# Cross attention's 154 keys in parts of 128 and 26 instead of 77 and 77

## The reference

```
qh = (x @ wq.T + bq).reshape(Bx, N, H, d).transpose(0, 2, 1, 3)
kh = (memory @ wk.T + bk).reshape(Bx, -1, H, d).transpose(0, 2, 1, 3)
vh = (memory @ wv.T + bv).reshape(Bx, -1, H, d).transpose(0, 2, 1, 3)
a = jax.nn.softmax(jnp.einsum('bhnd,bhmd->bhnm', qh, kh) / jnp.sqrt(jnp.float32(d)), axis=-1)
ca = jnp.einsum('bhnm,bhmd->bhnd', a, vh).transpose(0, 2, 1, 3).reshape(Bx, N, Cx)
ca = ca @ mha_out_w.T + mha_out_b
```

## Time and profile before

| | before |
|---|---|
| median of 3 runs | 1002.5 us (1002.33 to 1004.6) |
| the profiled execution | 1004.58 us |
| its span | 1002.8 us |
| mean granted TensorE clock | 0.853 of full speed |
| PE busy | 742.8 us, 74% |
| DVE busy | 562.2 us, 56% |
| ACT busy | 498.7 us, 50% |
| POOL busy | 297.2 us, 30% |

### The profile page before, as it was taken

One profiled execution on the slowest core, in us unless ns is written; L12 is line 12 of the kernel. 1 busy time (PEld: TensorE's weight loads), 2 busy tenths in 40 slices (PEclk: granted clock), 3 DMA queues, 4 the chain that ended last, 5 costly groups with the idle time before them and its releaser, 6 DMA issues.

```text
span 1002.8 us, 15716 instructions
## 1 busy us (share of the span) xinstructions
PE 742.8 (74%) x5368; PEld 489.7 (49%) x5368; DVE 562.2 (56%) x2206; ACT 498.7 (50%) x1315; POOL 297.2 (30%) x296
## 2 busy tenths in 40 slices
PE   5765487866786757699986686777757676768998
PEld 3444365544464635554444463555536455555543
DVE  5785455646654665635367555565555556464533
ACT  3436275574554545344544653755536354544443
POOL 3453314435232132130024242353333311331200
PEclk9877889888787888699998787798977988867999
DMA  8310010100100000042410101001010000002433
GB/s 288 111 38 1 11 39 1 48 2 11 38 2 11 1 1 2 14 126 77 142 37 1 37 7 42 1 11 38 1 47 2 11 1 2 1 1 61 114 97 96
DMA packets 35706, 39.47 MB, mean 39 GB/s; under 512 B 14169, under 2 KB 23467, under 8 KB 35499
## 3 DMA queue, kind: packets, MB, share of 16 engines
q1 hardware_dynamic: 35627, 38.47, 13.4%
HBM read 27.44 MB, written 1.57 MB: 29 GB/s over the span
## 4 chain that ended last, share of the span: by engine, by line
PE 46%; DVE 26%; ACT 17%; POOL 4%; issue 3%; DMA 1%; SPq 1%; DVEq 0%; POOLq 0%; ACTq 0%
ACT work L783 14%; PE act_psum L554 6%; PE moe_psum L564 5%; DVE work L1027 4%; PE dve_psum L421 4%; DVE work L1050 3%; PE dve_psum L390 3%; PE act_psum L634 3%; PE dve_psum L461 2%; PE dve_psum L637 2%; DVE res_nrm L1005 2%; DVE stats L996 2%; PE act_psum L451 2%; PE act_psum L527 2%; PE dve_psum L644 2%
## 5 line engine op out<-in xcount | busy, mean ns | idle before, releaser
L783 ACT ACTIVATE work<-work,nbias,rnorm 128x128 f32<-128x128 f32 x256 | 122.6, 480 | 75.1 <-DVE nbias L1087 75.0
L1384 POOL TENSOR_TENSOR work<-work,rinv 128x512 f32<-128x512 f32 (+1 forms) x80 | 84.7, 1076 | 249.7 <-DVE rinv L1014 249.7
L879 ACT ACTIVATE work<-act_psum,cols 128x512 f32<-128x512 f32 x80 | 54.6, 687 | 70.2 <-PE act_psum L554 70.2
L390 PE MATMUL dve_psum<-wqkv,hTs 128*128 128x512 f32 x128 | 72.3, 693 | 14.4 <-ACT hTs L905 13.8
L1366 POOL TENSOR_SCALAR rstd<-mv 128x4 f32<-128x4 f32 x36 | 10.1, 280 | 215.0 <-DVE mv L999 215.0
L1424 POOL TENSOR_TENSOR hT<-hT,work 128x512 f32<-128x512 f32 x32 | 40.6, 1270 | 108.5 <-DVE work L1050 108.4
L766 ACT COPY v_loc<-act_psum 77x512 f32<-77x512 f32 (+2 forms) x72 | 42.0, 583 | 61.3 <-PE act_psum L514 34.3
L1027 DVE CUSTOM_DVE_ANT_0 work<-dve_psum,masks 128x128 f32<-128x128 f32 x256 | 58.7, 285 | 23.2 <-PE dve_psum L421 23.2
L783 ACT ACTIVATE work<-work,nbias 128x154 f32<-128x154 f32 x128 | 52.3, 410 | 36.5 <-DVE nbias L1137 36.5
L766 ACT COPY hT<-act_psum 128x512 f32<-128x512 f32 (+1 forms) x60 | 31.0, 520 | 74.2 <-PE act_psum L451 35.4
L564 PE MATMUL moe_psum<-work,w_m 128*128 128x512 f32 x128 | 65.3, 598 | 1.0 <-DVE work L1193 1.0
(11 more groups left out here) (195 smaller groups left out, 1808.8 us busy)
## 6 DMA issues: line engine op xcount, KB each, us to landing
kT<-cwT_dram SPq DMA_DIRECT2D x160, 64.0 KB, 2.0
v_loc<-v_loc SPq DMA_DIRECT2D x24, 256.0 KB, 3.5
qT<-cwT_dram SPq DMA_DIRECT2D x96, 64.0 KB, 2.0
wqkv<-in_wqkv_dram SPq DMA_DIRECT2D x2, 768.0 KB
res_nrm<-in_x_dram SPq DMA_DIRECT2D x4, 256.0 KB, 2.9
w_m<-in_w_m_dram SPq DMA_DIRECT2D x1, 1024.0 KB, 9.1
v_loc<-v_loc SPq DMA_DIRECT2D x8, 128.0 KB, 3.1
shifted<-y SPq DMA_DIRECT2D x8, 128.0 KB
```

Of the source, the lines that this page charges most:

```text
L390: nc.tensor.matmul(bank[:], h, attn_w[:, k * INNER:(k + 1) * INNER], start=True, stop=True)\
L783: last = nc.scalar.activation(weights[:, i, :], weights[:, i, :], ACT.Exp, bias=nbias[u][:, b, i:i + 1], scale=scale_of(i), accum_out=sums ...
L879: nc.scalar.activation(dst, bank[:], ACT.Silu, bias=bias).then_inc(act_emptied, 1)
L1384: nc.gpsimd.tensor_tensor(some, some, by.unsqueeze(2).to_broadcast(list(some.shape)), ALU.mult).then_inc(ready[u], 1)
```

## The change

The keys of cross attention are cut at 128 (`P`) instead of 77 (`CH`); the rest is `REST` = 26.

- **Probabilities.** POOL and DVE divide keys 0 to 127 in place and write keys 128 to 153, divided, to `tail`, in which each head has 32 columns, six of them zero; four heads make one block of 128 columns. So each divides in two instructions.
- **Turning.** Eight transposes of 128x128, one for each head, and two of a whole `tail` block: ten instead of sixteen. The first four heads go to a DVE bank, the others and the two tails to two ACT banks.
- **Copies.** DVE makes one of 128x512, ACT one of 128x512 and one of 128x256.
- **Mix.** For each group of four heads four matmuls of 128 rows by 32 columns, then one of 128 rows by 128 columns with a block-diagonal value matrix (`v_tail`) that adds the last keys of all four heads.
- **Value matrix.** One matmul for the main part, eight of 26 output rows by 32 columns for the tail; DVE adds the bias in one and four instructions, after a memset of `v_tail`.
- **Scores.** DVE waits for all four banks, and takes part 0 of each first, then part 1, so that half a tile's heads are now the four of one part.

```diff
 def ca_turn_probs(t, u):
-    for g in range(2):
-        pe.wait_ge((probs_lo_ready, probs_hi_ready)[g][u], sm_cross(t))
-        for j, bank, filled in ((0, dve_bank(("pta_ca", t, u, g)), dve_filled),
-                                (1, act_bank(("ptb_ca", t, u, g)), act_filled)):
-            for i in range(4):
-                last = nc.tensor.transpose(bank[0:CH, i * P:(i + 1) * P],
-                                           prob[u][:, 4 * g + i, j * CH:(j + 1) * CH], ident[:])
-            last.then_inc(filled, 1)
+    for c in range(2):
+        pe.wait_ge((probs_lo_ready, probs_hi_ready)[c][u], sm_cross(t))
+        bank, filled = ((dve_bank, dve_filled), (act_bank, act_filled))[c]
+        bank = bank(("pt_ca", t, u, c))
+        for j in range(4):
+            last = nc.tensor.transpose(bank[:, j * P:(j + 1) * P], prob[u][:, 4 * c + j, 0:P], ident[:])
+        last.then_inc(filled, 1)
+    bank = act_bank(("tail_ca", t, u))
+    for c in range(2):
+        last = nc.tensor.transpose(bank[:, c * P:(c + 1) * P], tail[u][:, c, :, :].rearrange("p j k -> p (j k)"),
+                                   ident[:])
+    last.then_inc(act_filled, 1)
 
 def ca_mix(t, u):
-    pe.wait_ge(dve_emptied, dve_item["pta_ca", t, u, 1] + 1)
-    pe.wait_ge(act_emptied, act_item["ptb_ca", t, u, 1] + 1)
+    pe.wait_ge(dve_emptied, dve_item["pt_ca", t, u, 0] + 1)
+    pe.wait_ge(act_emptied, act_item["tail_ca", t, u] + 1)
     bank = act_bank(("oT_ca", t, u))
     for c in range(2):
-        for k, pt in enumerate((pta, ptb)):
-            for j in range(4):
-                part = slice(32 * j, 32 * j + 32)
-                v = slice(c * P + 32 * j, c * P + 32 * j + 32)
-                last = nc.tensor.matmul(bank[part, c * P:(c + 1) * P], v_ctx[u][:, k, v], pt[u][0:CH, 2 * j + c, :],
-                                        start=(k == 0), stop=(k == 1))
+        for j in range(4):
+            part = slice(32 * j, 32 * j + 32)
+            nc.tensor.matmul(bank[part, c * P:(c + 1) * P], v_main[u][:, c * P + 32 * j:c * P + 32 * j + 32],
+                             pta[u][:, 4 * c + j, :], start=True, stop=False)
+        last = nc.tensor.matmul(bank[:, c * P:(c + 1) * P], v_tail[u][:, c, :], tailT[u][:, c, :],
+                                start=False, stop=True)
     last.then_inc(act_filled, 1)
...
 def ca_take_scores(t, u):
-    for g in range(2):
-        for j in (2 * g, 2 * g + 1):
-            bank = filled(("s_ca", t, u, j))
-            for c in range(2):
-                i = 2 * j + c
-                last = mask_and_peak(bank, c * CTX, no_mask[:], prob[u][:, i, :], peak[u][:, 0, i:i + 1])
-            last.then_inc(dve_emptied, 1)
-        dve.wait_ge(dve_emptied, dve_item["s_ca", t, u, 2 * g + 1] + 1)
-        some = slice(HALF * g, HALF * g + HALF)
+    banks = [filled(("s_ca", t, u, j)) for j in range(4)]
+    for c in range(2):
+        for j in range(4):
+            i = 4 * c + j
+            last = mask_and_peak(banks[j], c * CTX, no_mask[:], prob[u][:, i, :], peak[u][:, 0, i:i + 1])
+            if c == 1:
+                last.then_inc(dve_emptied, 1)
+        if c == 0:
+            link(last)
+        else:
+            dve.wait_ge(dve_emptied, dve_item["s_ca", t, u, 3] + 1)
+        some = slice(HALF * c, HALF * c + HALF)
         nc.vector.tensor_scalar(nbias[u][:, 0, some], peak[u][:, 0, some], -CA_DH ** -0.5, None, ALU.mult)\
           .then_inc(peak_ready[u], 1)
...
     invert_sums(u, number, 0)
     dve.wait_ge(rinv_ready[u], half_done(number, 1))
-    some = prob[u][:, HALF:, :]
-    nc.vector.tensor_tensor(some, some, rinv[u][:, 0, HALF:].unsqueeze(2).to_broadcast([P, HALF, CTX]),
+    some, by = prob[u][:, HALF:, 0:P], rinv[u][:, 0, HALF:].unsqueeze(2)
+    nc.vector.tensor_tensor(some, some, by.to_broadcast([P, HALF, P]), ALU.mult)
+    nc.vector.tensor_tensor(tail[u][:, 1, :, 0:REST], prob[u][:, HALF:, P:], by.to_broadcast([P, HALF, REST]),
                             ALU.mult).then_inc(probs_hi_ready[u], 1)
...
 bank = dve_bank(("vc", u))
-for j in range(2):
-    last = nc.tensor.matmul(bank[0:CH, 2 * D * j:2 * D * (j + 1)], ctxT[u][:, j * CH:(j + 1) * CH], w_cav[:],
-                            start=True, stop=True)
+nc.tensor.matmul(bank[:, 0:2 * D], ctxT[u][:, 0:P], w_cav[:], start=True, stop=True)
+for c in range(2):
+    for j in range(4):
+        head = slice(c * P + 32 * j, c * P + 32 * j + 32)
+        last = nc.tensor.matmul(bank[32 * j:32 * j + REST, 2 * D + 32 * c:2 * D + 32 * c + 32], ctxT[u][:, P:CTX],
+                                w_cav[:, head], start=True, stop=True)
 last.then_inc(dve_filled, 1)
...
 bank = filled(("vc", u))
-nc.vector.tensor_tensor(v_ctx[u], bank[0:CH, :].rearrange("p (j n) -> p j n", j=2),
-                        row("bv_ca", 0, 2 * D, CH).unsqueeze(1).to_broadcast([CH, 2, 2 * D]), ALU.add).then_inc(dve_emptied, 1)
+nc.vector.tensor_tensor(v_main[u], bank[:, 0:2 * D], row("bv_ca", 0, 2 * D), ALU.add)
+link(nc.vector.memset(v_tail[u], 0.0))
+for j in range(4):
+    some, head = slice(32 * j, 32 * j + REST), slice(32 * j, 32 * j + 32)
+    last = nc.vector.tensor_tensor(v_tail[u][some, :, head], bank[some, 2 * D:2 * D + 2 * 32].rearrange("p (c n) -> p c n", c=2),
+                                   row("bv_ca", 0, 2 * D).rearrange("p (c n) -> p c n", c=2)[some, :, head], ALU.add)
+last.then_inc(dve_emptied, 1)
```

26 lines of the change are left out of this document (17 added, 9 removed).

## The result

The changed kernel takes 1012.7 us (median of four runs, 1011.0 to 1016.5) where the kernel before took 1002.6 beside it: a ratio of 1.010, interval 1.007 to 1.013. The forecast was 1000.1 us and the range ended at 1005.5, so the time lies outside it on the slow side. The profiled execution after took 1012.1 us, with a span of 1010.3.

The account below looks back on a forecast made before the run. The prediction took hand-overs between engines as the bound. Copies and division -4.2, turning -2.8, mix +3.8 and value matrix +0.8 summed to -2.4 us, taking the median 1002.5 to 1000.1 us, range 995.5 to 1005.5.

Parts of the forecast that it names:

- two kinds of round: Cross-attention tiles: the mix waits either on DVE's copies or on PE's own queue, 8 of 16 mixes each.
- the DVE kind: Rounds where DVE's pair of copies is the last piece before the mix; 8 of 16, each forecast 0.53 us shorter.
- The scores: DVE's wait for all four banks costs nothing; their release, 0.95 us later for PE, is covered by 3.37 us of exponentials.
- The mix: Three more changes of array shape per tile, about 0.3 us at the full clock: +3.8 us, bounds +2 to +6.
- it goes nowhere: Rival, chance 0.17: three shape changes cost 0.4 us, mix +5.5 and value matrix +1.5, so no change, 1002.5 us.
- Copies and division: One DVE copy fewer, -0.60 us, and a split division, +0.07, in eight DVE rounds: -4.2 us, bounds -3.6 to -4.8.
- Turning: Ten transposes for sixteen in PE rounds, half the gain left once the clock rises: -2.8 us, bounds 0 to -5.6.
- Value matrix: DVE's addition, memset and four small additions take 1.6 us per sample, mostly hidden: +0.8 us in all, 0 to +3.6.
- The clock rival: Rival, chance 0.18: fewer transposes keep PE less busy, so the lower clock lasts longer in PE rounds: 1006.7 us.
- a PE round: A tile's round whose mix follows PE's own queue, transposes then other PE work, without a gap; 8 of 16 mixes.
- A PE wait for a DVE bank that outlasts the exponentials: Sign of a wrong forecast: PE's wait for a late-released bank is longer than ACT's 3.37 us of exponentials.
- a first maximum well after the scores' end: Sign of a wrong forecast: DVE's first maximum, expected where PE's scores end, 0.83 us after they began, comes later.

Follow-up runs that it names:

- release_late: The kernel before, with the four scores banks released at maxima five to eight instead of two, four, six and eight: 1003.0 us against 1003.2, ratio 1.000.
- the fillers: Twelve transposes of the identity per tile ahead of the turning, work for nothing; with the new taking of scores added to the kernel before, 998.6 us.
- mix_mirrored: The changed kernel with the second group's tail matmul ahead of its four head matmuls (strips, full, full, strips): 1008.6 us, ratio 1.006 to the kernel before.
- old_order: The changed kernel with the scores taken as before, bank by bank, each released after its two maxima: 1007.2 us, ratio 1.004 to the kernel before.
- no_tail_mix_filled: The changed kernel with scores taken as before, the mix's two full matmuls left out, and twelve idle transposes a tile: 988.5 us, ratio 0.985 to the kernel before.
- before_filled: The kernel before with twelve idle transposes of the identity per tile ahead of the turning: 994.2 us against 1002.4, ratio 0.990.
- new_order_alone: The kernel before with only the new taking of the scores (four waits first, part 0 of all banks, then part 1): 1013.1 us against 1003.0, ratio 1.011.
- no_tail_mix: old_order without the two full matmuls of each mix, so the last 26 keys add nothing to the output: 995.2 us, ratio 0.991 to the kernel before.
- one_wait: The changed kernel, with DVE waiting once for the fourth scores bank instead of four times in a row: 1015.8 us, ratio 1.013 to the kernel before.
- old_order_mirrored: old_order with the second group's tail matmul ahead of its head matmuls in the mix: 1008.8 us, ratio 1.006 to the kernel before.
- old_order_filled: old_order with twelve idle transposes a tile ahead of the turning: 1000.6 us, ratio 0.995 to the kernel before; its runs fall near 992 and near 1001.
- waits_and_release: The kernel before with the waits for all four banks first and the late release together, maxima still bank by bank: 1013.8 us against 1002.8, ratio 1.010.

## Why the prediction was wrong, point by point

**What bounds the kernel.** Hand-overs, two kinds of round: it holds. What was missed is that the DVE kind is only safe while PE's step for the other sample is hidden by the exponentials, and how near its end is to showing: in the kernel before PE begins the turning 0.25 us after the last exponential.

**The scores: the step that failed.** The prediction put it at nothing, for two reasons. First, that the four banks come together because the first maximum starts where the scores end by the profile. They don't: four waits push it from 0.83 to 1.15 us. The rows before show DVE waiting on the first bank only, and the modelled end of PE's matmuls is no proof that the first semaphore and the fourth come at once. The Trainium skill, "TensorE: Matmul & The Clock Gate", Part 3, says that semaphore increments of matmuls packed side by side serialize; that the fourth bank shows 0.18 us after the first agrees in sign, but no run here separates it from the matmuls themselves. Second, that the late release is "covered by the 3.37 us of exponentials". Alone it is: release_late, 0.0 us. The two together are 1.2 us more of idle PE in one place, and there the cover ends, all the more where the step itself takes longer at the lower clock. Each edit was costed by itself against the same cover. Measured: +10.1 us for the part, where the sum had 0. How much of that is the later start and how much the lower clock isn't settled (the fillers took the part to 4.4 us).

**The mix: a term mis-sized.** Forecast three changes of shape at 0.11 us, 1.3 us from mix to scores and +3.8 us; measured 1.55. The rule "a full matmul costs as much as a strip group" holds at 128 columns too: 0.22 us in mix_mirrored against 0.22 in the earlier trace rows. What was too low is the change of shape. The 0.11 us came from one change in the earlier trace rows, from column strips to row strips, and was taken for all; from strips to full it is 0.14 and from full to strips or scores 0.20. With 0.54 us a tile (1.55 - 1.01) for the 0.3 it took, its +3.8 becomes +6.8, an estimate, beyond its upper bound of 6. The rival "it goes nowhere" had 0.4 for the three changes, nearer but still under 0.54.

**Copies and division: right in size and place.** old_order, where the order of scores is as before, shows them. Its second round goes from the first exponential to the mix in 8.02 us (329.90 to 337.92), and the kernel before in 8.53 (329.74 to 338.27): -0.51, forecast -0.53. The groups after by line and shape, busy time and mean ns behind the bar:

```profile
L1158 DVE COPY work<-dve_psum 128x512 f32<-128x512 f32 x16 | 10.9, 684 | 0.4
L1033 DVE TENSOR_TENSOR work<-work,rinv 128x512 f32<-128x512 f32 x16 | 11.1, 693 | 0.6
L1034 DVE TENSOR_TENSOR work<-work,rinv 128x104 f32<-128x104 f32 x16 | 4.2, 260 | 0.0
L1411 POOL TENSOR_TENSOR work<-work,rinv 128x104 f32<-128x104 f32 x16 | 5.7, 359 | 0.0
```

The copy goes by columns, as forecast (684 ns for 128 partitions, 680 for 77). DVE's two divisions hold 0.86 us of the chain in the second round (333.14 to 334.00), +0.06 over the 0.80 before; forecast +0.07. POOL's 104 elements take 0.36, forecast 0.37.

**Turning.** Ten transposes for sixteen, as forecast. What of the gain reaches the end wasn't isolated. no_tail_mix_filled is 5.7 us faster than before_filled, though it leaves out half of the old mix as well; half a mix, 0.44 us, on twelve tiles is 5.3 us. So copies, turning and value matrix together are worth about nothing, an estimate that carries the 5 us of before_filled's interval, where the sum had -4.2 - 2.8 + 0.8 = -6.2.

**Value matrix: right in size.** DVE after, the addition, the memset and the four small additions:

```profile
337.40 0.42 DVE L1284 TENSOR_TENSOR work<-dve_psum,rows 128x256 f32<-128x256 f32 x1
337.82 0.27 DVE L1285 MEMSET work<- 128x256 f32 x1
338.13 0.92 DVE L1288 TENSOR_TENSOR work<-dve_psum,rows 26x64 f32<-26x64 f32 x4
```

1.6 us from 337.40 to 339.05, as worked out. Its price alone wasn't tried.

**The clock rival: its mechanism came, beside the step that failed.** Its time, 1006.7, was nearer than the forecast, and the clock did stay down: 0.74 for 0.79. Both halves of the change do that, each without the other. new_order_alone (first line) has the new taking of the scores and all sixteen transposes; old_order (second line) has ten transposes and the scores taken as before:

```profile
308.00:420.00 112.00, 78.41 (x618) 61.06 (x619) 62.62 (x281) 51.43 (x170) 26.06 (x27) 0.72 0.01 4
```
```profile
308.00:420.00 112.00, 78.27 (x534) 52.83 (x532) 59.75 (x297) 50.71 (x173) 27.29 (x35) 0.73 0.01 4
```

no_tail_mix, with ten transposes and no full matmul in the mix, has 0.73 too, so the longer mix isn't needed for it; the fewer transposes and the split division weren't tried apart. In the fifth round of old_order, behind ten transposes, the eight records that take 3.60 us in the kernel before come out at the lower clock for a part of their time, in both stretches (the first shown, 4.41 us in the second):

```profile
378.95 4.47 PE L710 MATMUL act_psum<-hT,w_l 128*128 128x512 f32 x8
```

That is the rival's picture: a PE round in which the lower level lasts longer. release_late, with all sixteen transposes, has it in one stretch of two (4.91 us in the second), so ten transposes aren't the only way to it. The whole of old_order, 1007.2 us, even lies at the rival's time, but that is partly luck: its stretches are only 1.4 us longer than before's, and the mix's missing 3 us are in it. The rival didn't have the 10.1 us of the scores.

"A PE wait for a DVE bank that outlasts the exponentials" and "a first maximum well after the scores' end" stood in the list of what would show the prediction wrong; both came.

**What stays open.** The part of the span between the two stretches takes 381 to 386 us in kernels whose code for it is the same, and this is as large as several of the differences above. It hid the gains of one_wait and of old_order_mirrored; no run separates its reason. With it counted out, the mirrored mix takes 4.1 us off the stretches of the changed kernel (216.2 against 220.3), 1.7 off old_order's and 3.8 off old_order_filled's. Also open are how the new order's loss divides between clock and waiting, and the two clusters of old_order_filled.

## What to carry to other kernels

Two edits that each lean on the same cover must be costed together: 0.3 us later and 0.9 us later were 7.6 and 0 us alone, and 11.0 together. Where a wait for many buffers replaces waits for one at a time, count the time to the last buffer and each wait that is added, and ask what PE does meanwhile: behind an idle stretch, or behind less work, its next step can run at the lower clock. Price each change of the array's shape from a row of that very change. And when a small edit's effect is missing from the total, look at the stretch where it acts before calling it nothing: here parts of equal code differed by up to 5 us.

## What the hardware showed that was not expected

- A longer idle time ahead of a step of PE went with a longer step: 32 records in 3.81 us after 0.71 or 1.61 us of idle, in 5.44 after 1.94. It isn't the idle time alone, since in waits_and_release the same 32 kept 3.81 us after 1.94 in one stretch and took 5.44 in the other.
- Twelve useless transposes a tile took 8.2 us off the kernel before and raised the granted clock of its first stretch from 0.79 to 0.88. The Trainium skill, "TensorE: Matmul & The Clock Gate", Part 4, says that the full clock doesn't engage for transposes, which don't count as busy in the same way. These runs speak against it: the fillers are transposes and nothing else. So do old_order and no_tail_mix, where six transposes fewer went with 0.73 for 0.79.
- Four waits in a row on DVE took 0.14 us more than one wait on the last bank (1.15 against 1.01 us from the scores' start to the first maximum).
- A full matmul of 128 columns between strip groups takes 0.42 us, but 0.22 behind another full one, as a strip group of four does: the change of shape costs 0.14 us one way and 0.20 the other.
